# Scratch rows of a gated feed-forward kernel, laid out by weight tile and loaded with one transfer each

## The reference, cut to what matters

```python
    def _L0_cond_ref(u, length, log_dt, C, log_A_real, A_imag, D):
        ...
        y = jnp.fft.irfft(u_f * k_f, n=n)[..., :Lq]
        y = y + u_m * D[:, None]
        return y * mask[:, None, :]

        def dequant_gptq(qweight, scales, zeros, groupsize):
            ...
            q = qweight[k // PACK, :] >> (k % PACK * 4)[:, None] & 15
            ...
            return q.astype(jnp.float32) * s[g] - zp[g]
        ...
        gate = x2 @ Wg
        up = x2 @ Wu
        inter = gate * jax.nn.sigmoid(gate) * up
        out = (inter @ Wd).astype(jnp.float16)
```

## Time and profile before

| | us |
|---|---|
| median of 3 runs | 1215.04 |
| lowest, highest | 1213.88, 1215.89 |
| the profiled execution | 1214.16 |
| its span | 1212.4 |

### The profile page before, as it was taken

One profiled execution on the slowest core, in us unless ns is written; L12 is line 12 of the kernel. 1 busy time (PEld: TensorE's weight loads), 2 busy tenths in 40 slices (PEclk: granted clock), 3 DMA queues, 4 the chain that ended last, 5 costly groups with the idle time before them and its releaser, 6 DMA issues.

```text
span 1212.4 us, 15497 instructions
## 1 busy us (share of the span) xinstructions
PE 1168.9 (96%) x5546; PEld 953.3 (79%) x5546; DVE 893.1 (74%) x961; ACT 852.3 (70%) x1398; POOL 208.0 (17%) x121
## 2 busy tenths in 40 slices
PE   4998999999999999999999999999999999999995
PEld 4898998688788788888788678788788787887873
DVE  7788724477777777777777788787777777777777
ACT  5532203988788788788787877778787887887862
POOL 0021100121111211211211851211211211211110
PEclk8898999999999999999999999999999999999996
DMA  8665867434434434334334255545334334334423
GB/s 290 234 234 183 288 210 245 119 98 103 117 94 115 109 92 120 104 96 122 103 91 112 64 189 143 177 154 159 105 91 120 102 96 120 98 103 112 142 70 139
DMA packets 148018, 165.61 MB, mean 137 GB/s; under 512 B 24854, under 2 KB 111062, under 8 KB 147686
## 3 DMA queue, kind: packets, MB, share of 16 engines
q1 hardware_dynamic: 147910, 164.59, 46.2%
q0 software_dynamic: 32, 0.03, 0.0%
HBM read 155.74 MB, written 11.64 MB: 138 GB/s over the span
## 4 chain that ended last, share of the span: by engine, by line
PE 89%; DVE 6%; DMA 1%; issue 1%; SPq 1%; ACT 1%; POOL 0%; DVEq 0%
PE pair L1097 27%; PE pair L1132 26%; PE pair L1114 25%; PE pair L1057 9%; DVE acc L905 1%; PE pair L1017 1%; DMA x_fin<-in_x_dram 1%; DVE p L662 1%; DVE y_nat L811 0%; PE pair L1037 0%; DMA u_all<-in_x_dram 0%; DVE s_r L662 0%; SPq L395 0%; PE pair L1147 0%; DVE q_in L916 0%
## 5 line engine op out<-in xcount | busy, mean ns | idle before, releaser
L905 DVE SCALAR_TENSOR_TENSOR acc<-pair,s_down,acc 128x1024 f32<-128x1024 f32 x336 | 430.6, 1283 | 214.3 <-PE pair L1132 213.7
L605 ACT ACTIVATE pair<-pair,ratio 128x512 f32<-128x512 f32 x616 | 383.3, 668 | 114.9 <-PE pair L1097 114.8
L624 ACT ACTIVATE pair<-pair,ratio 128x512 f32<-128x512 f32 x588 | 365.2, 661 | 131.3 <-PE pair L1114 131.3
L1097 PE MATMUL pair<-xs,wg 128*128 128x512 f32 x1408 | 390.4, 399 | 2.7 <-DVE sil L884 2.7
L1114 PE MATMUL pair<-xs,wu 128*128 128x512 f32 x1344 | 370.3, 397 | 2.0 <-DVE sil L889 1.9
L1097 PEld LDWEIGHTS pair<-xs,wg 128*128 128x128 f32 x1408 | 263.8, 189 | 69.3 <-ACT pair L605 7.4
L1114 PEld LDWEIGHTS pair<-xs,wu 128*128 128x128 f32 x1344 | 249.2, 189 | 70.2 <-issue 11.9
L1132 PE MATMUL pair<-mid_h,wd 128*128 128x512 f32 x704 | 278.5, 400 | 5.4 <-DVE acc L905 3.5
L1132 PE MATMUL pair<-mid_l,wd 128*128 128x512 f32 x672 | 266.6, 397 | 0.0
L492 POOL CAST mid_h<-sil 128x1024 fp32r<-128x1024 f32 (+1 forms) x44 | 46.3, 1051 | 858.4 <-DVE sil L889 843.3
L1132 PEld LDWEIGHTS pair<-mid_h,wd 128*128 128x128 f32 x704 | 133.8, 192 | 43.9 <-DVE acc L905 9.7
(11 more groups left out here) (146 smaller groups left out, 379.8 us busy)
## 6 DMA issues: line engine op xcount, KB each, us to landing
q_in<-rows_backwards SPq DMA_DIRECT2D x672, 64.0 KB, 2.3
z_in<-zeros_plus_one SPq DMA_DIRECT2D x130, 256.0 KB, 4.6
toep<-kernel_padded SPq DMA_DIRECT2D x64, 512.0 KB, 5.9
q_in<-_L_ffn_down_qweight_dram SPq DMA_DIRECT2D x42, 512.0 KB, 5.7
u_all<-in_x_dram SPq DMA_DIRECT2D x16, 512.0 KB, 8.9
x_fin<-in_x_dram SPq DMA_DIRECT2D x12, 512.0 KB, 8.1
out_dram<-x_fin SPq DMA_DIRECT2D x12, 512.0 KB, 6.9
q_in<-in_x_dram SPq DMA_DIRECT2D x4, 512.0 KB, 5.8
```

The lines of the kernel that those rows point to most:

```text
L605: act.activation(gate_ps[:, tb, :], gate_ps[:, tb, :], ACT.Copy, scale=ratio[:, 0, G * t + g:G * t + g + 1]).then_inc(gate_scaled, 1)
L624: act.activation(up_ps(tau)[:, tb, :], up_ps(tau)[:, tb, :], ACT.Copy, scale=ratio[:, 1, G * t + g:G * t + g + 1]).then_inc(up_scaled, 1)
L905: dve.scalar_tensor_tensor(out=acc[:, hid, :], in0=ps, scalar=scale, in1=acc[:, hid, :], op0=ALU.mult, op1=ALU.add).then_inc(down_taken, 1)
L1097: mm = pe.matmul(gate_ps[:, tb, :], w["g"][tau % 2][:, g, :], xs[:, part, g, 512 * tb:512 * tb + 512], start=g == 0 and part == 0, stop=pa ...
```

## The change

The scratch gets the shape of the tiles: 21 gate tiles, 21 up tiles and one tail tile, each 16 word rows x 8 groups x 128 words, so that a tile is one block in the order in which it is loaded. A gate or up load is then one transfer of 128 partitions x 1024 words (4096 bytes in a row). The copies to the scratch change with it: for each r and each of gate and up there is one copy of 21 tiles x 8 groups x 128 words (512 bytes in a run) and one for the tail of 8 groups x 64 words, 64 copies in all, and the wait before the first load is for 64. DVE's count of parts (`q_due`) follows. Down loads, zeros, order and waits stay.

```diff
-    rows_back = nc.dram_tensor("rows_backwards", (2, HID // PACK, INTER), I32, kind="Internal").ap()
+    rows_back = nc.dram_tensor("rows_backwards", (2 * TAIL + 1, 16, G, P), I32, kind="Internal").ap()
...
                 for e, q in ((0, gq), (1, uq)):
-                    sp.dma_start(bass.AP(rows_back.tensor, (e * (HID // PACK) + 15 - r) * INTER,
-                                         [[16 * INTER, G], [INTER // 2, 2], [1, INTER // 2]]),
-                                 bass.AP(q.tensor, r * INTER, [[16 * INTER, G], [INTER // 2, 2], [1, INTER // 2]])
+                    sp.dma_start(rows_back[e * TAIL:e * TAIL + TAIL, 15 - r],
+                                 bass.AP(q.tensor, r * INTER, [[P, TAIL], [16 * INTER, G], [1, P]])
+                                 ).then_inc(rows_back_in, 16)
+                    sp.dma_start(rows_back[2 * TAIL, 15 - r, :, M_TAIL * e:M_TAIL * e + M_TAIL],
+                                 bass.AP(q.tensor, r * INTER + P * TAIL, [[16 * INTER, G], [1, M_TAIL]])
                                  ).then_inc(rows_back_in, 16)
...
-                elif t == TAIL:
-                    for e in range(2):
-                        for g in range(G):
-                            sp.dma_start(q_in[slot][:, g, M_TAIL * e:M_TAIL * e + M_TAIL],
-                                         bass.AP(rows_back.tensor, e * (HID // PACK) * INTER + P * t + rows * g,
-                                                 [[INTER, 16], [0, PACK], [1, M_TAIL]])
-                                         ).then_inc(q_loaded[slot], 16)
                 else:
-                    e = "gu".index(m)
-                    for g in range(G):
-                        sp.dma_start(q_in[slot][:, g, :],
-                                     bass.AP(rows_back.tensor, e * (HID // PACK) * INTER + P * t + rows * g,
-                                             [[INTER, 16], [0, PACK], [1, P]])
-                                     ).then_inc(q_loaded[slot], 16)
+                    tile_at = 2 * TAIL if t == TAIL else "gu".index(m) * TAIL + t
+                    sp.dma_start(q_in[slot][:].rearrange("p g n -> p (g n)"),
+                                 bass.AP(rows_back.tensor, tile_at * 16 * G * P, [[G * P, 16], [0, PACK], [1, G * P]])
+                                 ).then_inc(q_loaded[slot], 16)
...
-                    sp.wait_ge(rows_back_in, 16 * 32)
+                    sp.wait_ge(rows_back_in, 16 * 64)
...
-                parts = (1 if m == "d" else G) * (1 + is_tail(tau)) + 1
+                parts = 1 + (m == "d" and is_tail(tau)) + 1
```

More of the change, by code:

```diff
@@ L374, in load_weights @@
                 loads += 1
-                rows = 16 * INTER
                 if m == "d" and t == TAIL:
```

## The result

| us | before | after |
|---|---|---|
| median (19 runs each) | 1215.04 | 1212.83 |
| the profiled execution | 1214.16 | 1213.94 |
| its span | 1212.4 | 1212.2 |

The ratio is 0.9976, 95% interval 0.9968 to 0.9985: the change makes the kernel faster by 2.2 us in the medians and by 1.8 to 3.9 us in the ratio. One of the 19 executions after took 1447.89 us at a granted clock of 0.746 and is left out of the ratio. The two profiled executions differ by only 0.2 us, so a pair of profiles doesn't show the gain by its span; it has to be looked for place by place.

A forecast was written before the change was run, and what follows sets the result against it. TensorE, busy 1168.9 us of a 1212.4 span, was taken as the bound. Steady part 0, SP 0, scratch 0 and change of halves -0.7 gave a median of 1214.3 us (1213.5 for a profiled execution), range 1212.0 to 1217.5.

The forecast's parts named there:

- the steady loads: Gate and up loads of the projections: one transfer instead of eight pieces, cost and gain 0.
- the x transfers of the change of halves: DVE's wait for x_fin near 786: x lands sooner behind lighter rings, -0.7 us, ends 0 and -1.0.
- the second wait: DVE's other wait for x_fin, 1.6 us, said to leave no gap on TensorE.
- The lighter rings: Ahead of x at the change of halves: 256 and some 50 KB off the rings, 1.0 us at 315 GB/s.
- rival (3): Over 206 to 221 us, lighter rings give time back to ACT: 2.7 us, 1211.6; chance 0.06.
- the scratch copies: At convolution groups 0 to 7, 64 copies instead of 32: cost 0, up to several us at the upper end.
- the second rival: In the convolution, copies overload half the engines and Toeplitz loads come late: 1217.5 to 1228, likeliest 1220; chance 0.10.
- My price for an old copy: From window 107 to 108: a run of 5504 bytes costs 265 ns, 13% more per byte; 16 runs a copy.
- the margin of 0.9 us ahead of the store: On SP, group 1's copies end at 67.9, ahead of the store at 68.77; called the narrowest margin.
- The sign that I had named: The forecast is wrong if the store at 68.8 comes later by a us or more.
- (1): Nothing reaches TensorE: x is late because of the stores and loads around it; 1215.0, chance 0.10.
- the DMA share and the packets: Profile after: DMA share of a steady period near 0.35, and some 74,000 packets fewer.

The follow-up runs named there:

- e3: Changed kernel, but gate and up tiles 24 to 30 still loaded in pieces; 1215.61 us, ratio 1.0007.
- e2: New scratch layout, one transfer per load only for gate and up tiles 24 to 30, pieces elsewhere; 1212.99 us, ratio 0.9978.
- e5: New scratch layout, one transfer per load only for up tiles 27 and 28, issued right ahead of the late x transfers; 1212.42 us, ratio 0.9984.
- e6: New scratch layout, one transfer per load only for gate tiles 28 and 29, issued right behind the late x transfers; 1216.15 us, ratio 1.0011.
- e9: Kernel before, with the zeros of up tiles 27 and 28 issued ahead of their eight pieces; 1211.39 us, ratio 0.9979.
- e1: Kernel before with only the new scratch layout and its 64 copies, loads still in pieces; 1214.82 us, ratio 0.9999.
- e10: Changed kernel with every scratch copy issued a second time into a spare array, 128 copies; 1243.41 us, ratio 1.0247.
- e7: Kernel before, with x for rows 4 to 7 issued earlier, behind the gate load of its tile; 1211.66 us, ratio 0.9976.
- e8: Changed kernel, with x for rows 4 to 7 issued earlier, behind the gate load of its tile; 1212.85 us, ratio 0.9982.

## Why the prediction was right, and where it was not

**Right: the steady loads are free.** The margin was there (24 us from issue to use in both), and e3, with 72 of the 86 loads changed, has a ratio of 1.0007. SP's waiting on the centering grew from some 380 us to 780. The estimate of over 1200 us in the prediction used a figure that the Trainium skill (page "DMA: Bandwidth & Descriptors", section "Anatomy of one DMA") gives for transfers issued from GpSimd. These are issued from SP, and no run here shows a cost of that size.

**Right: the place and the mechanism of the gain.** It was forecast at the x transfers of the change of halves, through the rings being lighter ahead of x, by the zeros and the last pieces. e2, e3, e5 and e6 put it there and ahead of x, and e9, within that, on the zeros.

**Wrong: the size of that term.** I took -0.7 us with ends 0 and -1.0; the medians give -2.2, and e2 -2.3. The step that failed was reading one execution as the typical one. I wrote that the second wait leaves no gap on TensorE. It was 1.60 us in that execution, and in e1, e3 and e6, which load the same way ahead of x, it was 3.0 to 3.2, after a first one of 3.1. Put side by side, the waits show a threshold: 1.35 (e2) and 1.60 cost nothing, 2.42 costs 0.70 us of start, 3.13 costs 1.42, and the 0.52 + 3.00 of e1's second place cost 1.89. TensorE has 1.6 to 1.7 us of margin and loses what goes beyond, plus 0.1 in the round behind the gap. That is 1.42 + 1.89 + 0.2 = 3.5 us in e1 and 0.8 in before's profile; the measured 2.2 lies between. How often an execution of before waits like the one or like the other was not measured. A 1.60 us wait with no gap behind it was one that had just used up its cover, and should have widened the term to both places.

The lighter rings were undersized too: I forecast x to land 1.0 us sooner, by bytes over bandwidth. At the first place it took 7.96 us and not 9.83 (before) or 10.54 (e1); at the second 7.66 and not 8.68 or 10.67. Only the pair 8.68 and 7.66 differs by what I forecast, and why the rest differ by twice that is open. My chance of 0.84 for a change within 0.2% was therefore too high: the ratio's centre, 0.9976, lies just outside, and its interval on both sides of the bound. The range of 1212.0 to 1217.5 held with 0.8 us to spare, and that was partly luck: its lower end came from the spread of three runs and from rival (3), which did not happen, and not from the ends of this term.

**Right in the sum, off in the parts: the scratch copies.** They cost nothing (e1 0.9999). By the window 109 to 110 above, where only copies drain, a run of 512 bytes from DRAM to DRAM costs 0.51 x 16 / 295 = 27.7 ns, below my 33 and far below the 71 at which the second rival decides.

My price for an old copy was misread. The window 107 to 108 in the earlier trace rows does not hold old copies alone: SP issued the store of z_one at 104.97, and its 256-byte runs drain there too. Nor is an old copy 16 runs: the page of before counts 148018 - 147686 = 332 packets of 8 KB and more, that of e1 153618 - 153542 = 76. So two half rows went as one run of 11,008 bytes, 8 to a copy, and by the packet records such a run took 413 ns. The 265 ns and the 13% are wrong. My 33 ns took them in, but the cost of 0 did not hang on it.

The number of engines can be counted from packets. The pages of before and of e1:

```profile
DMA packets 148018, 165.61 MB, mean 137 GB/s; under 512 B 24854, under 2 KB 111062, under 8 KB 147686
...
DMA packets 153618, 165.61 MB, mean 136 GB/s; under 512 B 25334, under 2 KB 116918, under 8 KB 153542
```

Per period of the projections the trace of before has 320 packets of 4 bytes for its 20 transfers on 16 engines, and that of after 96 for six: each engine that takes part in a transfer leaves one. From before to e1, which differ in the copies alone, the packets under 512 bytes grow by 25334 - 24854 = 480. Of these 256 are the tail's runs, and the other 224 are 7 for each of the 32 additional copies. The rule of the Trainium skill (page "DMA: Bandwidth & Descriptors", section "Why a DMA increments its semaphore by 16 and not by 1"), seven engines for an outer dimension of 21 and eight for one of 8, agrees with that count; with my eight it would be 512. The share of 0.51 could not have told seven from eight.

On SP I was too low. The copies of the tail took 0.65 and not 0.46, so a group took 6.0 us and not 5.2, and the margin of 0.9 us ahead of the store was used up:

```profile
63.94 0.78 SPq L362 DMA_DIRECT2D rows_backwards<-_L_ffn_gate_qweight_dram  x1
64.76 0.66 SPq L365 DMA_DIRECT2D rows_backwards<-_L_ffn_gate_qweight_dram  x1
...
69.25 0.71 DVE L794 TENSOR_TENSOR k_sb<-k_sb,d_row 32x8 f32<-32x8 f32 x1
...
69.30 0.65 SPq L365 DMA_DIRECT2D rows_backwards<-in_L_ffn_up_qweight_dram  x1
69.99 0.44 SPq L313 DMA_DIRECT2D kernel_padded<-k_sb  x1
...
72.91 1.77 SPq L322 DMA_DIRECT2D toep<-kernel_padded  x4
...
DMA to landing us min/median/max: 3.8/6.0/11.0
```

The store itself was not held up: the copies end at 69.95 and DVE has the kernel words ready at 69.96, 1.2 us later than in before like the rest of this execution. The sign that I had named, a store that comes later by a us or more, came up without its cause. From the store to the Toeplitz loads it is 2.9 us here, and 2.0 in before (68.77 to 70.74), with the copies issued right ahead of the store still in the rings. The loads of group 4 went out that 0.9 us later and still came in time: TensorE has no gap in the convolution but the one at 111, for DVE. e10 shows the other side of this cover.

**The rivals.** (1), nothing reaches TensorE, falls with e2 and e9. (2), the scratch copies make it slower, falls with e1; it needed 71 to 96 ns per run and the runs took 27.7, and e10 shows that SP, not the rings, would have been the way to lose there. (3), ACT gets time back from 206 to 221: the share of the rings fell from 0.67 to 0.60, there are 55 matmul records where there were 54, and e3 has no gain. It falls.

**Wrong, without consequence: the DMA share and the packets.** I had 0.35 for a steady period; it stayed at 0.41. The 60 us of engine time that 2048 pieces of 512 bytes took in a period now belong to 256 rows of 4096 bytes, so a row costs 235 ns. My 175 came from a stretch of Toeplitz loads, and a row costs more in the steady part: there the rows of the down loads took 245 ns already in before, by the packet records. Packets fell by 83,396 and not by some 74,000. The rest are nearly all of the 4-byte kind: 618 transfers fewer x 16, less 32 copies more x 7, is 9,664; for the old copies I had counted 256 too many.

## What to carry to other kernels

Where the bound engine is busy throughout, thousands of small transfers can be free, and one large one at the wrong place in the queue is not: look for a burst (here stores and reloads between weight loads) and ask what stands ahead of its last member. Moving the zeros of two tiles ahead of their words (e9), or issuing x earlier (e7), gave what 618 fewer transfers gave. The queue of the issuing engine counts beside the DMA engines: in before, eight small issues put the zeros behind them off by 5.1 us (767.24 to 772.30), with the DMA engines at 0.33 meanwhile. A wait that just fits its cover in the profiled execution is a cost in others: price it from that cover, at every place where the pattern occurs, and take a second profile before trusting a term of a microsecond.

## What the runs showed of the hardware

- A copy from DRAM to DRAM in runs of 512 bytes costs 27.7 ns per run, about what a load into SBUF in such pieces costs (29.4), and the DMA share while only such copies drained was 0.51 with an outer dimension of 21.
- In this kernel's transfers each engine that takes part leaves one packet of 4 bytes (320 per period for 20 transfers on 16 engines; 96 for six). By that count a copy with an outer dimension of 21 ran on seven engines (224 packets for 32 copies, e1 against before).
- Two half rows of 5504 bytes that follow each other were moved as one run of 11,008 bytes, in 413 ns (before).
- An issue on SP took 0.77 us for 168 runs, and 0.65 for 8 runs of the tail from DRAM to DRAM, where 8 runs from DRAM to SBUF took 0.46.
- Executions of one kernel here spread over 3 to 10 us (1210.83 to 1214.03 in twelve runs of e8, 1210.47 to 1220.18 in 35 of before). In the profiles a good part of that arises ahead of 50 us and around the pass from one half to the other, along with differences in TensorE's granted clock: over 0 to 40 us it was 0.83 in the first profile of after, 0.87 in that of before and 0.91 in e9's. What sets it differently each time was not found.
